# One power on GpSimd for both layer norms of a slot, and the gate's hidden layer in pairs of tiles

## The reference

```python
x = einsum('oc,bchw->bohw', inv(I - circulant(ricker_filter)), x)     # 128x128 mix of channels
t = tokens(x)                                                         # 16 x 1024 x 128
t = t + linear_attention(layernorm(t))    # 8 heads of 16, elu+1 features, causal, W_q W_k W_v W_out
z = layernorm(t)
gh = relu(z @ gfc1_w.T + gfc1_b)          # the gate's hidden layer: 128 wide, for every token
g = (gh @ gfc2_w.T + gfc2_b).mean(tokens) # 8 gates for each batch
W1m, b1m, W2m, b2m = base + sum_e g[e] * task_vector[e]               # merged for each batch
t = t + layernorm_affine(z + relu(z @ W1m.T + b1m) @ W2m.T + b2m)
```

## Time and profile before

| | |
|---|---|
| median of 3 runs | 760.04 us (759.29 to 769.75) |
| profiled execution, its own time | 759.07 us |
| its span | 757.2 us |
| mean granted TensorE clock | 0.978 |
| busy in the span: PE, DVE, ACT, POOL | 92%, 87%, 85%, 71% |
| first phase | to 503.9 us: about 470 us with all stages, then the pipeline drains |
| second phase | 503.9 us to the end; POOL is busy for three tenths of it |

### The profile page before, as it was taken

One profiled execution on the slowest core, in us unless ns is written; L12 is line 12 of the kernel. 1 busy time (PEld: TensorE's weight loads), 2 busy tenths in 40 slices (PEclk: granted clock), 3 DMA queues, 4 the chain that ended last, 5 costly groups with the idle time before them and its releaser, 6 DMA issues. The chain is left out here.

```text
span 757.2 us, 39181 instructions
## 1 busy us (share of the span) xinstructions
PE 696.7 (92%) x12194; PEld 548.2 (72%) x12194; DVE 655.9 (87%) x2361; ACT 646.9 (85%) x1860; POOL 534.7 (71%) x1167
## 2 busy tenths in 40 slices
PE   4898999999999999999999999868999998999993
PEld 2576777777777777777777777766777787777772
DVE  5797989999999999999999999647989878898983
ACT  4788999999999999999999999436888886888883
POOL 3798999999999999999999999310333321333333
PEclk9999999999999999999999999689999999999997
DMA  5656766656656656656656655310122220222221
GB/s 152 114 122 131 139 118 149 143 123 150 144 122 151 144 121 152 144 120 152 145 119 153 144 120 109 69 46 2 58 78 75 83 71 26 74 83 83 83 83 71
DMA packets 202486, 82.68 MB, mean 109 GB/s; under 512 B 176092, under 2 KB 189823, under 8 KB 202376
## 3 DMA queue, kind: packets, MB, share of 16 engines
q1 hardware_dynamic: 202440, 82.08, 47.1%
HBM read 22.79 MB, written 17.30 MB: 53 GB/s over the span
## 5 line engine op out<-in xcount | busy, mean ns | idle before, releaser
L875 DVE SCALAR_TENSOR_TENSOR scores_lo<-p_a,scores_hi 128x512 f16<-128x512 f32 x256 | 175.1, 684 | 6.8 <-ACT scores_hi L773 2.1
L773 ACT ACTIVATE scores_hi<-p_a 128x512 f16<-128x512 f32 x256 | 161.8, 641 | 7.3 <-PE p_a L614 7.1
L1419 POOL TENSOR_TENSOR ffn_rstd_shift<-ffn_rstd_shift,consts 128x4 f32<-128x4 f32 x32 | 36.8, 1150 | 111.2 <-DVE ffn_rstd_shift L1377 111.2
L984 POOL CAST qk_parts<-qk_f 128x256 f16<-128x256 f32 x256 | 108.7, 427 | 3.2 <-DVE qk_f L852 2.0
L994 POOL TENSOR_TENSOR qk_parts<-qk_f,qk_parts 128x128 f16<-128x128 f32 x256 | 103.8, 426 | 0.9
L1355 DVE TENSOR_TENSOR h_lo<-h_f,h_hi 128x512 f16<-128x512 f32 x128 | 95.9, 789 | 0.6 <-ACT h_hi L1257 0.6
L1201 PE MATMUL psb<-merged_W_of_batch,h_hi 128*128 128x128 f16 x512 | 94.2, 220 | 2.3 <-DVE h_lo L1355 1.5
L1203 PE MATMUL psb<-merged_W_of_batch,h_lo 128*128 128x128 f16 x512 | 93.8, 219 | 0.0
L1202 PE MATMUL psb<-merged_W_of_batch,h_hi 128*128 128x128 f16 x512 | 93.8, 219 | 0.0
L1246 ACT ACTIVATE h_f<-psb,merged_b_of_batch 128x512 f32<-128x512 f32 x128 | 87.1, 713 | 7.6 <-PE psb L1182 6.0
L631 PE MATMUL p_o<-v_parts,scores_hi 128*128 128x17 f16 x1024 | 90.1, 171 | 1.4
(11 more groups left out here) (215 smaller groups left out, 2824.5 us busy)
## 6 DMA issues: line engine op xcount, KB each, us to landing
x_f<-in_x SPq DMA_DIRECT2D x32, 256.0 KB, 3.2
t_rows<-t SPq DMA_DIRECT2D x64, 128.0 KB, 2.3
t_back<-t_rows SPq DMA_DIRECT2D x32, 256.0 KB, 2.6
out<-out_tile SPq DMA_DIRECT2D x32, 256.0 KB, 2.0
tv_share<-in_L_ffn_tv_W SPq DMA_DIRECT2D x32, 128.0 KB, 2.2
qkT_parts<-qk_parts SPq DMA_TRANSPOSE x128, 3.1
zT_hi_lo<-z_parts SPq DMA_TRANSPOSE x128, 2.3
merged_W<-in_L_ffn_W SPq DMA_DIRECT2D x2, 256.0 KB, 4.6
```

The source lines that it names most:

```text
L773: nc.scalar.activation(ah[:, t % 2, cols], p_a[:, cols], ACT.Relu).then_inc(ahi_ready[eo], 1)
L875: nc.vector.scalar_tensor_tensor(al[:, t % 2, cols], p_a[:, cols], 0.0, ah[:, t % 2, cols], ALU.max, ALU.subtract).then_inc(alo_ready[eo], 1)
L984: nc.gpsimd.tensor_copy(dst, src.unsqueeze(2).broadcast_to([P, NH, 2, DH])).then_inc(done, 1)
```

## The change

It does three things, all in the first phase.

1. **One power for both norms.** `st` and `st2` become the two halves of one tile `sts`. `rsqrt` (POOL, skew 1, first in the slot) waits for `mv1` of tile n and `mv2` of tile n-7 and raises two columns at once, one of each half; the semaphores `rstd1` and `rstd2` become one, `rstd`. So that both variances lie at the same place of their halves, the second norm's statistics of tile t move to place (t+3)%4. The first seven slots raise one column; the last seven tiles' second norms are done by `last_rsqrt2`, one column each, in the draining slots.
2. **The gate's products for two tiles.** `gate` does nothing for even tiles; at every odd one it multiplies both: three products of 256 columns, in twice the room of `p_m2`.
3. **The gate's relu for two tiles.** `gate_relu` follows with one activation of 256 columns and one accumulator output for each pair; `ghs` has 64 columns in place of 128, and `gate_ready` counts pairs.

```diff
-GPSIMD_ORDER = [("rsqrt1", 1), ("z_hi", 10), ("split_x", 0), ("q_hi", 2), ("z_lo", 10), ("k_hi", 2), ("rsqrt2", 8),
+GPSIMD_ORDER = [("rsqrt", 1), ("z_hi", 10), ("split_x", 0), ("q_hi", 2), ("z_lo", 10), ("k_hi", 2), ("last_rsqrt2", 8),
                 ("qk_lo", 2)]
...
+                    def reads(read, b, t, ahead):
+                        if read is gate_ready:
+                            return TILES // 2 * b + (t + ahead) // 2
+                        return TILES * b + t + ahead
...
                     def gate(b, t):
+                        if t % 2 == 0:
+                            return
                         n = TILES * b + t
-                        pe.wait_ge(z_turned[t % 4], 32 * b + 16 * (t // 4 + 1))
-                        bank_read("gate", n)
-                        g = p_m2[:, P:2 * P]
-                        hi, lo = zh[:, bass.ds(n * P, P)], zl[:, bass.ds(n * P, P)]
-                        mm(g, gfh[:, :], hi, start=True, stop=False)
-                        mm(g, gfl[:, :], hi, start=False, stop=False)
-                        mm(g, gfh[:, :], lo, start=False, stop=True).then_inc(gt_done, 1)
+                        for tile in (t - 1, t):
+                            pe.wait_ge(z_turned[tile % 4], 32 * b + 16 * (tile // 4 + 1))
+                        bank_read("gate", b, t)
+                        g, cols = p_m2[:, P:3 * P], bass.ds((n - 1) * P, 2 * P)
+                        mm(g, gfh[:, :], zh[:, cols], start=True, stop=False)
+                        mm(g, gfl[:, :], zh[:, cols], start=False, stop=False)
+                        mm(g, gfh[:, :], zl[:, cols], start=False, stop=True).then_inc(gt_done, 1)
...
                     def gate_relu(b, t):
-                        n = TILES * b + t
+                        if t % 2 == 0:
+                            return
+                        m = TILES // 2 * b + t // 2
...
-                        act.wait_ge(gt_done, n + 1)
-                        nc.scalar.activation(gjunk[:, :], p_m2[:, P:2 * P], ACT.Relu, bias=gf1b[:, 0:1], scale=1.0 / WS,
-                                             accum_out=ghs[:, bass.ds(n, 1)]).then_inc(gate_ready, 1)
+                        act.wait_ge(gt_done, m + 1)
+                        nc.scalar.activation(gjunk[:, :], p_m2[:, P:3 * P], ACT.Relu, bias=gf1b[:, 0:1], scale=1.0 / WS,
+                                             accum_out=ghs[:, bass.ds(m, 1)]).then_inc(gate_ready, 1)
...
                     def shift2(b, t):
                         n = TILES * b + t
-                        dve.wait_ge(rstd2, n + 1)
+                        dve.wait_ge(rstd, n + 1 + PAIRED)
...
-                    def rsqrt1(b, t):
-                        n = TILES * b + t
-                        s = st[:, t % 4, :]
+                    def rsqrt(b, t):
+                        n = TILES * b + t
+                        both = not isinstance(n, int) or n >= PAIRED
                         pool.wait_ge(mv1, n + 1)
-                        nc.gpsimd.tensor_tensor(s[:, RSTD:RSTD + 1], s[:, VAR:VAR + 1], mhalf, ALU.pow).then_inc(rstd1, 1)
-
-                    def rsqrt2(b, t):
-                        n = TILES * b + t
-                        s = st2[:, t % 4, :]
+                        if both:
+                            pool.wait_ge(mv2, n - PAIRED + 1)
+                        s = sts[:, 0:2 if both else 1, t % 4, :]
+                        nc.gpsimd.tensor_tensor(s[:, :, RSTD], s[:, :, VAR], mhalf[:, 0:2 if both else 1], ALU.pow)\
+                            .then_inc(rstd, 1)
+
+                    def last_rsqrt2(b, t):
+                        n = TILES * b + t
+                        if not isinstance(n, int) or n < NT - PAIRED:
+                            return
+                        s = st2[:, (t + 3) % 4, :]
                         pool.wait_ge(mv2, n + 1)
-                        nc.gpsimd.tensor_tensor(s[:, RSTD:RSTD + 1], s[:, VAR:VAR + 1], mhalf, ALU.pow).then_inc(rstd2, 1)
+                        nc.gpsimd.tensor_tensor(s[:, RSTD:RSTD + 1], s[:, VAR:VAR + 1], mhalf[:, 0:1], ALU.pow)\
+                            .then_inc(rstd, 1)
```

More of the change, by code:

```diff
@@ L391, in build @@
             zp = sb(pa_, "z_parts", [P, 4, 2, C], F16)
-            st = sb(pa_, "stats1", [P, 4, 16])
-            st2 = sb(pa_, "stats2", [P, 4, 16])
+            sts = sb(pa_, "stats", [P, 2, 4, 16])
+            st, st2 = sts[:, 0], sts[:, 1]
             dn = sb(pa_, "denominators", [P, 2, 2, NH])
-            gjunk = sb(pa_, "gate_hidden", [P, P])
+            gjunk = sb(pa_, "gate_hidden", [P, 2 * P])
             tvs = sb(pa_, "tv_share", [P, 2, TVW])
@@ L405, in build @@
             sbank = p_s[:, 0:NP * 2 * VW].rearrange("p (a w) -> p a w", w=2 * VW)
-            (conv_done, in_done, bn1, mv1, rstd1, vhi_ready, exp_ready, relu_ready, vlo_ready,
+            (conv_done, in_done, bn1, mv1, rstd, vhi_ready, exp_ready, relu_ready, vlo_ready,
              qk_ready, qhi_ready, khi_ready, lo_ready, su_done, state_cleared, sh_ready, sp_ready,
              av_done, den1, den2, o_ready, ot_done, oT_ready, wo_done,
-             t1_ready, bn2, mv2, rstd2, shift_ready, z_ready, zhi_ready, zlo_ready, gt_done, gate_ready) = [
+             t1_ready, bn2, mv2, shift_ready, z_ready, zhi_ready, zlo_ready, gt_done, gate_ready) = [
                 sem(s) for s in (
-                    "conv_done in_done bn1 mv1 rstd1 vhi_ready exp_ready relu_ready vlo_ready "
+                    "conv_done in_done bn1 mv1 rstd vhi_ready exp_ready relu_ready vlo_ready "
                     "qk_ready qhi_ready khi_ready lo_ready su_done state_cleared sh_ready sp_ready "
                     "av_done den1 den2 o_ready ot_done oT_ready wo_done "
-                    "t1_ready bn2 mv2 rstd2 shift_ready z_ready zhi_ready zlo_ready gt_done gate_ready").split()]
+                    "t1_ready bn2 mv2 shift_ready z_ready zhi_ready zlo_ready gt_done gate_ready").split()]
             sc_done, ahi_ready, alo_ready = [[sem(f"{name}_{eo}") for eo in range(2)] for name in
@@ L541, in bank_read @@
                         assert 2 * TILES - dict(TENSOR_ORDER)[stage] - before(stage, previous) + 1 > 0
-                        if isinstance(n, int):
+                        if isinstance(b, int):
                             for other, read in uses.items():
                                 for s_ in read:
-                                    at_least(pe, s_, cap(n - before(stage, other) + 1))
+                                    ahead = min(1 - before(stage, other), NT - TILES * b - t)
+                                    at_least(pe, s_, reads(s_, b, t, ahead))
                         else:
                             for s_ in uses[previous]:
-                                pe.wait_ge(s_, n - before(stage, previous) + 1)
+                                pe.wait_ge(s_, reads(s_, b, t, 1 - before(stage, previous)))
                     def conv(b, t):
@@ L647, in turn_out @@
                         pe.wait_ge(o_ready, n + 1)
-                        bank_read("turn_out", n)
+                        bank_read("turn_out", b, t)
                         nc.tensor.transpose(p_m2[:, 0:P], o_[:, t % 2, :], ident).then_inc(ot_done, 1)
@@ L907, in mean_var2 @@
                         dve.wait_ge(bn2, upto)
-                        nc.vector.bn_aggr(st2[:, t % 4, MEAN:MEAN + 2], st2[:, t % 4, 0:9]).then_inc(mv2, 1)
+                        nc.vector.bn_aggr(st2[:, (t + 3) % 4, MEAN:MEAN + 2], st2[:, (t + 3) % 4, 0:9]).then_inc(mv2, 1)
                     nc.vector.memset(st[:, :, 6:8], 0.0)
@@ L1020, in split_x @@
                             .then_inc(xl_ready, 1)
[L1022 removed]
+                    run(pool, GPSIMD_ORDER, {"rsqrt": rsqrt, "qk_lo": qk_lo,
                         "split_x": split_x,
[L1024 removed]
+                        "last_rsqrt2": last_rsqrt2, "q_hi": qk_hi(0, qhi_ready), "k_hi": qk_hi(1, khi_ready), "z_hi": z_hi, "z_lo": z_lo})
         with ExitStack() as pb:
@@ L1290, in link @@
                         dve.wait_ge(b_chain, n[0])
-                    nc.vector.tensor_reduce(gsum[:, :], ghs[:, :].rearrange("p (b t) -> p b t", t=TILES), AX.X, ALU.add)\
+                    nc.vector.tensor_reduce(gsum[:, :], ghs[:, :].rearrange("p (b t) -> p b t", t=TILES // 2), AX.X, ALU.add)\
                         .then_inc(gs_ready, 1)
```

33 lines of the change are left out of this document (15 added, 18 removed).

## The result

The changed kernel takes 779.87 us (median of 4 runs, 773.08 to 784.15) where the kernel before, on the same chip, takes 762.07 (4 runs). The ratio is 1.021, with an interval of 1.017 to 1.025: slower, where 731 was forecast. The profiled execution took 773.08 us, its span is 771.3 and its mean granted clock 0.931.

A forecast was written before the change was run, and what follows sets the result against it. GpSimd was taken as the bound at 3.561 us a slot; loads of 3.22 to 3.29 after gave a slot of 3.32, 0.24 less on 110 slots (26.4 us), with the drain 28.4: from 759.07 to 731, range 717 to 752.

The forecast's parts named there:

- The power's price: GpSimd's two-column power: 0.75 us long, pitch 0.70 in place of 1.01 for two powers, saving 0.31 a slot.
- Rival 3: GpSimd's second power column almost free, GpSimd at 3.05 a slot, slot 3.25, 723 us; chance 0.10.
- rival 4: Columns 64 elements apart make GpSimd's power dearer, pitch 1.20, GpSimd 3.75 a slot, 778 us; chance 0.05.
- rival 2: On GpSimd two columns cost as two powers, pitch near 1.0; only the drain gains 2 us, 757; chance 0.11.
- GpSimd comes first: First phase: GpSimd, busy 99.01% with no idle time, sets the pace at 3.561 us a slot.
- these waits cost nothing: TensorE's turn_out waits for the relu (8.4 us), the relu for the products (4.1); costless while GpSimd sets the pace.
- I apply that ratio: ScalarE's work over busy time, 0.965, applied to VectorE and TensorE, giving 3.25 and 3.29 us a slot.
- ScalarE's own work: ScalarE's pitches without waits: 3.34 us a slot before; after, even 3.08, odd 3.23, with task vectors 3.22 on average.
- The wait added by the pair: Gate's products end 0.16 us later in TensorE's even slots; the forecast's sum had no term for the relu's wait.
- Rival 1: TensorE and ScalarE's lock step at the gate becomes the bound: odd slots 3.23 + 0.5, mean 3.47, 747 us; chance 0.14.
- both of its signs: Relu's wait for products longer than 0.3 us in every odd slot, and batch above 27.5 us (3.44 a slot).
- The drain: From slot 136 on, pairs remove two of four waits of the gate's products: 2.3 us, taken as 2.

The follow-up runs named there:

- two powers: Changed kernel with the paired gate's products and relu one slot later, and two powers of one column each again: 752.2 us, ratio 0.986.
- power alone: Kernel before with one power of two columns for both norms, the gate still per tile: 762.3 us, ratio 0.998.
- gate alone: Changed kernel with two powers of one column each again, the gate still in pairs: 779.8 us, ratio 1.022.
- gate before project: Changed kernel with gate ahead of project in TensorE's order: 762.3 us, ratio 0.999.
- task vectors in slot 3: Changed kernel with the split of the task vectors in slot 3 of each batch in place of slot 2: 762.6 us, ratio 0.998.
- 748.1 kernel: Changed kernel with the paired gate's products and relu one slot later (skews 14 and 15): 748.1 us, ratio 0.980.

## Why the prediction was wrong

- **The power's price was right.** 0.75 us forecast, 0.70 measured; pitch 0.70 and 0.65. Rival 3, the almost free second column, is out: it would have left the power near 0.55. Its source in the Trainium skill (GPSIMD Engine Reference, "Elementwise — side-by-side cycle accounting") measured an add, and for this power the trace decides. Nor was it dear: with 64 elements between the columns the pitch is 0.65, where rival 4 needed more than 1.03 and rival 2 about 1.0.
- **"GpSimd comes first"** was half right. It was at its floor within 1% (28.08 with two powers, 28.36 before), but it did not stand alone. The power by itself moved the batch by nothing. The rows said so: `turn_out` waited for the relu and the relu for the products, and I wrote that these waits cost nothing while GpSimd sets the pace. The power alone shows that there was another bound, and these waits are the likeliest.
- **"I apply that ratio"** is a step of the sum that no run bears out. Busy time times 0.965 gave 3.29 for TensorE, a load that let the slot be put at 3.32, a batch of 26.6. The shortest batch of any kernel is near 27.85, 3.48 a slot, and TensorE is busy for 26.94 us of it, 3.37 a slot; no kernel brought that under 3.34. So 3.29 came from a ratio read on another engine, and whether TensorE's work can be packed as densely is not shown. VectorE's busy time, 26.25 or 3.28 a slot in that kernel, is near the 3.25 forecast. ScalarE's own work, which had been added up from pitches, came out as forecast: 3.09 in the even slot (3.08), and in the odd one 4.03 less 0.70 before the relu and 0.09 before `read_t1`, 3.24 (3.23).
- **The wait added by the pair was left out of the sum**, and this is the step that turned the sign. The forecast averaged ScalarE's 3.08 and 3.23 to 3.22 and gave the relu's wait nothing. Rival 1 had the place (products that end 0.16 later in the even slot, relu of the odd one), and both of its signs came: the relu waits longer than 0.3 in every odd slot, and the batch is above 27.5. But its price of 747 was 33 us short. It put the odd slot at 3.23 + 0.5 = 3.73; measured are 4.03 to 4.26. Read as the prediction read it, from `read_t1` to the relu (303.82 to 304.67) less 0.15, the idle time is 0.70, where 0.5 was kept and 0.44 is the mean of the odd slots before; another 0.1 to 0.2 stands ahead of `read_t1`. The even slot lost the 0.34 of its relu, as rival 1 and the forecast both had it, but the gain went into the longer wait behind it. TensorE's even slot starts by the round (`relu_qk`, `make_qk`, `divide`, `turn_out` or `split_x`, `x_lo`, `conv`, then to the gate), so the length of two slots is that chain's and not the sum of what ScalarE does in them.
- **The clock** stood nowhere in the working. The earlier trace rows show 1.00, and I took it as given. A batch with a fall lost 1.33 us by it; rival 1 had no such term either.
- **The drain** was undersized: 2 us forecast, 7.5 measured. With pairs the products wait 0.18 us for the relu and 0.37 for a DMA there, where they waited 1.51 and three times 1.13 for the relu. That the pairs do it is shown: from the last full slot to the gate's last relu it is 36.6 and 36.0 us in the kernels without pairs (before, power alone) and 29.1 to 30.0 in those with pairs (after, gate alone, gate before project). The clock is 0.79 on average in the drain before and 0.90 after, but its share is small: with pairs, 0.94 (gate alone) and 0.89 (task vectors in slot 3) give 29.6 and 29.9.

What stays open: why the clock falls in some batches of a kernel and not in others that look the same; why it stood at 0.95 between the falls in the profiled execution of the changed kernel; and what bounds the 748.1 kernel, in which no engine is busy for more than 97%. A batch at 0.95 took 29.42, at 1.00 in the kernel with the gate alone 29.32, so by an estimate it cost about 0.1 a batch, if the power costs that kernel nothing.

## What to carry to other kernels

Before an edit that relieves an engine at 99%, look for waits that two other engines put on each other: they can be a bound of their own, and then the gain ends there. When work of two steps is merged into one, the merged piece takes the place of one of them, and it should go where its producer starts early and its consumer has no wait: here one slot's shift was worth 32 us and decided the sign. An engine's slot that gets shorter is no gain if the wait in the next slot takes it back: compare rounds, not slots. And do not shrink busy time by a ratio taken from another engine; add up that engine's own pitches.

## What the runs showed of the hardware

- The power on GpSimd: 548 ns for one column of 128 partitions, 698 for two, 1150 for four; a pitch of 0.65 for two.
- In the changed kernel TensorE's granted clock fell to half for 3 to 4 us with no idle time longer than 0.29 us before it in its slot; in the 3.5 us ahead of one fall TensorE was busy for 2.79. In the 748.1 kernel it waits up to 0.76 us for a DMA, and the clock stays at 1.00:

```profile
302.33 0.40 PE L618 MATMUL p_a<-qkT_parts 64*128 64x128 f16 x8 [0.76 <-DMA qkT_parts<-qk_parts]
```

- Where the fall came, a batch paid 1.33 us, and moving one instruction of half a microsecond on each of two other engines by one slot took all of them away (no fall in the last twelve batches).
